# Causal feature-map scores in 64x64 array tiles: only the query columns at or after each 64-key block, new PSUM banks and engine orders

## The reference

```python
x = x + tanh(g_xattn) * performer(layernorm(x), ctx, ctx)
x = x + tanh(g_ffn) * ffn(layernorm(x))
```

```python
num[t] = sum(k'[s] . q'[t] * v[s] for s <= t)
den[t] = sum(k'[s] . q'[t] for s <= t)
out[t] = num[t] / den[t]
```

## Time and profile before

| | |
|---|---|
| median of 3 runs | 1070.0 us (1068.78 to 1070.27) |
| span of the profiled execution, first to last instruction | 1067.6 us |
| TensorE busy | 1012.6 us, 95% |
| VectorE busy | 961.4 us, 90% |
| ScalarE busy | 758.7 us, 71% |
| GpSimd busy | 752.5 us, 70% |
| TensorE's mean granted clock | 0.997 of full |
| HBM read, written | 28.23 MB, 8.39 MB |

### The profile page before, as it was taken

One profiled execution on the slowest core, in us unless ns is written; L12 is line 12 of the kernel. 1 busy time (PEld: TensorE's weight loads), 2 busy tenths in 40 slices (PEclk: granted clock), 3 DMA queues, 4 the chain that ended last, 5 costly groups with the idle time before them and its releaser, 6 DMA issues.

```text
span 1067.6 us, 32201 instructions
## 1 busy us (share of the span) xinstructions
PE 1012.6 (95%) x12870; PEld 831.4 (78%) x12870; DVE 961.4 (90%) x2176; ACT 758.7 (71%) x1564; POOL 752.5 (70%) x1111
## 2 busy tenths in 40 slices
PE   1568999999999999999999999999999999999998
PEld 0447788788888888888888888888888888888787
DVE  7778888999999999999999999999999999998996
ACT  6678877776677777668777666877766687776541
POOL 4578877787677778767778766777876677787531
PEclk9989999999999999999999999999999999999999
DMA  9501000011000001100100100010111000000000
GB/s 311 169 21 31 12 24 29 31 31 31 23 28 25 22 31 31 32 21 24 29 22 32 32 31 22 21 32 21 32 32 31 22 22 31 22 21 12 12 11 30
DMA packets 38915, 38.67 MB, mean 36 GB/s; under 512 B 3440, under 2 KB 38512, under 8 KB 38768
## 3 DMA queue, kind: packets, MB, share of 16 engines
q1 hardware_dynamic: 38384, 36.59, 10.9%
q0 software_dynamic: 384, 0.04, 0.0%
HBM read 28.23 MB, written 8.39 MB: 34 GB/s over the span
## 4 chain that ended last, share of the span: by engine, by line
PE 87%; DVE 5%; POOL 4%; issue 1%; ACT 1%; DMA 0%; SPq 0%; POOLq 0%; DVEq 0%; ACTq 0%
PE ps L2302 15%; PE ps L2304 14%; PE ps L2303 14%; PE ps L2333 10%; PE ps L2348 9%; PE ps L2341 5%; PE ps L2317 5%; PE ps L2382 3%; PE ps L2373 3%; PE ps L2296 2%; PE ps L2358 2%; DVE hk L1770 2%; PE ps L2366 1%; PE ps L2367 1%; PE ps L2325 1%
## 5 line engine op out<-in xcount | busy, mean ns | idle before, releaser
L1434 DVE SCALAR_TENSOR_TENSOR z<-ps,gate,z 128x256 f32<-128x256 f32 x512 | 238.5, 472 | 37.9 <-PE ps L2304 29.0
L2302 PE MATMUL ps<-we_hi,h_hi 128*128 128x512 f32 (+2 forms) x640 | 240.5, 376 | 0.6 <-DVE z L1434 0.4
L2304 PE MATMUL ps<-we_hi,h_lo 128*128 128x512 f32 (+2 forms) x640 | 224.1, 350 | 0.0
L2303 PE MATMUL ps<-we_lo,h_hi 128*128 128x512 f32 (+2 forms) x640 | 223.7, 349 | 0.0
L2302 PEld LDWEIGHTS ps<-we_hi,h_hi 128*128 128x128 f32 x640 | 120.4, 188 | 36.7 <-issue 12.6
L2333 PE MATMUL ps<-qf,kf 64*128 64x256 f32 x1024 | 129.2, 391 | 9.1 <-POOL kf L549 4.5
L2304 PEld LDWEIGHTS ps<-we_hi,h_lo 128*128 128x128 f32 x640 | 120.2, 188 | 17.1
L2303 PEld LDWEIGHTS ps<-we_lo,h_hi 128*128 128x128 f32 x640 | 120.8, 189 | 11.5
L2333 PEld LDWEIGHTS ps<-qf,kf 64*128 64x128 f32 x1024 | 96.4, 191 | 29.8 <-issue 11.3
L2348 PE MATMUL ps<-att,v 128*32 128x256 f32 (+1 forms) x2048 | 109.0, 329 | 3.1 <-POOL att L540 0.9
L911 ACT ACTIVATE att<-ps 128x512 f32<-128x512 f32 x32 | 19.1, 597 | 116.8 <-PE ps L2333 116.7
(11 more groups left out here) (232 smaller groups left out, 3079.7 us busy)
## 6 DMA issues: line engine op xcount, KB each, us to landing
x_in<-in_x SPq DMA_DIRECT2D x32, 256.0 KB, 2.6
c_in<-in_ctx SPq DMA_DIRECT2D x32, 256.0 KB, 2.6
out<-z SPq DMA_DIRECT2D x32, 256.0 KB, 2.2
c_chunk<-in_ctx SPq DMA_DIRECT2D x14, 512.0 KB, 8.0
stage<-in_L_ffn_We SPq DMA_DIRECT2D x2, 1024.0 KB, 10.0
c_chunk<-in_ctx SPq DMA_DIRECT2D x2, 256.0 KB, 6.5
stage_b<-in_L_ffn_bup SPq DMA_DIRECT2D x1, 256.0 KB, 6.9
stage_q<-in_L_ffn_Wq SPq DMA_DIRECT2D x1, 256.0 KB, 6.4
```

Source lines behind the costliest of these rows:

```text
L1434: return dve.scalar_tensor_tensor(out=z[b % 2][:, t, :], in0=ps[:, bank, offset:offset + D], scalar=gate[:, t, ex:ex + 1], in1=z[b % 2][:, ...
L2302: pe.matmul(out, a_hi(c), b_hi(c), start=(c == 0), stop=False)
L2303: pe.matmul(out, a_hi(c), b_lo(c), start=False, stop=False)
L2304: last = pe.matmul(out, a_lo(c), b_hi(c), start=False, stop=(c == C - 1))
```

## The change

Tokens of a batch lie as two blocks of 128. In the key block 1 the halves are exchanged: partitions 0 to 63 hold keys 192 to 255, partitions 64 to 127 keys 128 to 191. The loads of the context do that (`keys_of`, and three transfers per chunk instead of one), and the triangle `causal` is built to match. `first_keys` and `second_keys` become one function `scores`, called for X00, X01, X11 and X10; Y0 and Y1 are gone. Each matmul takes 64 keys as weights and only the queries from the first of these keys on, in a 64x64 tile whose column half is the one in which its keys lie. Score columns that are no longer written are cleared once (`clear_`), and multiplied away or masked. `BANK` is new throughout, so are all orders and the assignment of steps to semaphores, and many waits now stand only for the batches in which they are written out. `a00_` to `a12_` become two steps each (`a00_` and `b00_`).

```diff
-            def first_keys(b, oct, step, *banks):
+            def scores(oct, step, own_banks, last_banks):
                 for j in range(2):
-                    for half in range(2):
-                        r, pr = slice(M * half, M * half + M), 4 * oct + 2 * step + j
-                        last = pe.matmul(ps[:, banks[half], j * L:(j + 1) * L], kf[r, pr, 0:P], qf[r, pr, :],
-                                         start=True, stop=True)
-                return last
-
-            def second_keys(b, oct, *banks):
-                for j in range(4):
-                    for half in range(2):
-                        r, pr = slice(M * half, M * half + M), 4 * oct + j
-                        last = pe.matmul(ps[:, banks[half], j * P:(j + 1) * P], kf[r, pr, P:L], qf[r, pr, P:L],
-                                         start=True, stop=True)
+                    pr, q = 4 * oct + 2 * step + j, (2 * step + j) * P
+                    for c in range(2):
+                        for half in range(2):
+                            r, k = slice(M * half, M * half + M), M * c
+                            pe.matmul(ps[M * c:M * c + M, own_banks[half], j * L + k:(j + 1) * L], kf[r, pr, k:k + M], qf[r, pr, k:L],
+                                      start=True, stop=True, tile_position=(M * half, M * c))
+                    for c in (1, 0):
+                        for half in range(2):
+                            r, k = slice(M * half, M * half + M), M * (1 - c)
+                            last = pe.matmul(ps[M * c:M * c + M, last_banks[half], q + k:q + P], kf[r, pr, P + M * c:P + M * c + M], qf[r, pr, P + k:L],
+                                             start=True, stop=True, tile_position=(M * half, M * c))
                 return last
...
+            def X11_(b):
+                pe.wait_ge(*at("x000", b))
...
+                if b in (0, 1, 5):
+                    pe.wait_ge(*at("x001", b))
+                scores(1, 1, (BANK["x110"], BANK["x111"]), (BANK["y10"], BANK["y11"])).then_inc(*up("X11", b))
...
+            def X10_(b):
+                pe.wait_ge(*at("x011", b))
+                pe.wait_ge(*at("y00", b))
+                scores(1, 0, (BANK["x100"], BANK["x101"]), (BANK["y10"], BANK["y11"])).then_inc(*up("X10", b))
...
@@ hn_t_
-                if b + 1 < NB:
-                    pe.wait_ge(*at("y10", b + 1))
+                if b >= 1:
+                    pe.wait_ge(*at("ssub", b - 1))
@@ fkp_
+                if b == 5:
+                    pe.wait_ge(*at("a13", b - 5))
                 if b >= 5:
-                    pe.wait_ge(*at("a01", b - 5))
+                    pe.wait_ge(*at("b01", b - 5))
@@ banks
-BANK = dict(stab=0, fk0=6, fk1=4, fk2=3, fk3=7, fq0=0, fq1=2, fq2=4, fq3=1, x000=3, x001=1, x010=0, x011=5,
-            y00=3, y01=7, av0=3, x100=0, x101=2, x110=5, x111=4, y10=1, y11=6, av1=2, nd0=2, nd1=0, ht=1,
-            dn=7, qq=1, kv0=7, kv1=5, s=7, pv0=0, pv1=1, otr=4, o=1, h20=3, h21=6, mm0g=3, mm1g=6, mm00=5,
-            mm01=3, mm02=5, mm03=5, mm10=4, mm11=6, mm12=2, mm13=5, first=0)
+BANK = dict(av0=0, av1=3, dn=5, first=0, fk0=0, fk1=6, fk2=4, fk3=5, fq0=2, fq1=3, fq2=7, fq3=4, h20=1, h21=0, ht=2,
+            kv0=2, kv1=6, mm00=4, mm01=0, mm02=7, mm03=7, mm0g=1, mm10=5, mm11=6, mm12=3, mm13=6, mm1g=0, nd0=2,
+            nd1=3, o=7, otr=4, pv0=1, pv1=2, qq=7, s=2, stab=0, x000=1, x001=7, x010=2, x011=4, x100=4, x101=5,
+            x110=3, x111=7, y00=5, y01=0, y10=1, y11=6)
@@ loads
+        def keys_of(dram, b, c):
+            return dram[b, :, :].rearrange("(q p) d -> p q d", p=M)[:, c:4 - c:3 - 2 * c, :]
...
-                sp.dma_start(c_in[b % 2][:, :, :], rows(ctx_d, b)).then_inc(*c_load.up(b))
+                for c in range(2):
+                    sp.dma_start(c_in[b % 2][M * c:M * c + M, :, :], keys_of(ctx_d, b, c)).then_inc(*c_load.up(b))
...
-                sp.dma_start(c_chunk[(b + 1) % CHUNK_BUFFERS][:, 0:n * T, :], rows(ctx_d, at_, n)).then_inc(*ctx_in.up(b))
+                held = c_chunk[(b + 1) % CHUNK_BUFFERS][:, 0:n * T, :].rearrange("p (b t) d -> p b t d", t=T)
+                src = ctx_d[at_:at_ + n, :, :].rearrange("b (q p) d -> p q b d", p=M)
+                sp.dma_start(held[:, :, 0, :], ctx_d[at_:at_ + n, 0:P, :].rearrange("b p d -> p b d")).then_inc(*ctx_in.up(b))
+                for c in range(2):
+                    sp.dma_start(held[M * c:M * c + M, :, 1, :], src[:, 3 - c]).then_inc(*ctx_in.up(b))
@@ gated sums, one of six
-                gated(b, 0, 0, BANK["mm00"], 0).then_inc(*up("a00_", b))
-                dve.wait_ge(*at("a00_", b))
-                gated(b, 0, 1, BANK["mm00"], D).then_inc(*up("a00", b))
+                gated(b, 0, 0, BANK["mm00"], 0).then_inc(*up("a00", b))
+
+            @per_batch
+            def b00_(b):
+                dve.wait_ge(*at("a00", b))
+                gated(b, 0, 1, BANK["mm00"], D).then_inc(*up("b00", b))
@@ once, on VectorE
+            def clear_():
+                for bank in sorted(set(range(8)) - {BANK[f"f{of}{j}"] for of in "kq" for j in range(4)}):
+                    last = dve.memset(ps[:, bank, :], 0.0)
+                last.then_inc(*up("clear"))
```

2045 lines of the change are left out of this document (1084 added, 961 removed).

## The result

The changed kernel takes **1104.6 us** (median of 4 runs, 1101.9 to 1105.4); the kernel before, beside it, 1069.8 (1068.8 to 1070.3). The ratio is **1.0322, 95% interval [1.0308, 1.0337]**: 3.2% slower, where 1050.6 us and a gain of 1.8% were forecast.

What follows compares the result with a forecast made beforehand. TensorE was taken to bound the middle, with VectorE nearest. Gains of 15.6 (24 periods), 3.2 (seven before) and 0.65 (last block) made 19.4 us off the 1067.6 us span; plus 2.4 outside it, 1050.6 us, range 1038 to 1065.

Steps and rivals of the forecast that it cites:

- The other blocks of TensorE keep their matmuls ... nothing: TensorE outside the score block: same matmuls, seven changes of tile shape before and after, so no change in time.
- a gain of 19.4 us: Whole span: 15.6 us from 24 periods, 3.2 from the seven before them, 0.65 from the last block.
- X11, `hn_t` and the feature products had cover: Three places in each period where a possible wait was said to be covered by 0.2 to 0.5 us.
- `hn_t`'s cover of 0.5 us: New wait of `hn_t` on `ssub`, sharing bank 2: VectorE's chain ends at 9.7 us, `hn_t` stands at 10.27.
- The premise behind the sum: 24 middle batches: TensorE's savings shorten the 31.22 us period until another engine blocks, nearest VectorE at about 29.8.
- The sum of the score block: X00's start to `av0`: 4.45 + 0.1 + 0.25 + 0.2 = 5.0 us against 5.64, gain used 0.65 a batch.
- (b): Score block: tiles of unequal length do not run four wide, 0.85 us a batch slower, 1097 us; chance 0.08.
- (c): Score block: weight loads show, 1.75 us a batch, net 1.1 us slower, 1105 us; chance 0.02.
- The start: Up to the first score block: 34 more SyncE transfers, booked at 0, bounds -1 and +3 us.
- a first score block after 43 us: Sign that the forecast is wrong; the first score block was expected within 38 to 42 us.
- The fill: Seven periods before the steady ones: 7 x 0.65 x 0.7 = 3.2 us gained.
- Rival (a): Each period: waits eat part of the gain, 0.48 us left, 1055.5 us; 1070 if nothing is left; chance 0.13.

Runs made afterwards that it cites:

- new_order_wide_tiles: Changed kernel with its new orders, banks and loads, but scores again in two-wide tiles of 128 keys: 1123.5 us, ratio 1.0512.
- x_in_three: Changed kernel with three buffers for x instead of two, its load waiting for `x1` of three batches back: 1097.8 us, ratio 1.0263.
- tiles_in_old_order: Kernel before with only the four-wide score tiles, exchanged key halves and two-transfer key loads, old orders and banks kept: 1070.3 us, ratio 1.0012.
- one_load_a_chunk: Changed kernel with each chunk of keys for the norms loaded by one transfer instead of three, halves exchanged once afterwards: 1101.7 us, ratio 1.0306.
- start_vector_list: Changed kernel with one transfer per chunk and the hand-written start lists of GpSimd and VectorE reordered: 1094.7 us, ratio 1.0246.
- masks-first runs: GpSimd's masks moved ahead of `v_bd` in the old orders, with the new tiles and in the kernel before: 1102.2 and 1101.5 us.

## Why the prediction was wrong

**The step that failed** is the price of what else was changed: "The other blocks of TensorE keep their matmuls ... nothing", with no loss booked for waits and 0 for the start. It priced new orders, banks and waits by counting work. With the loads and the start they cost 52.7 us of span with the old tiles (new_order_wide_tiles), 19.6 of it in the 24 periods, against a gain of 19.4 us that the forecast made of the tiles. The prediction listed where X11, `hn_t` and the feature products had cover, and named no chain ahead of X00. There the bias add, the copy of v and `k_lo` (1.27 + 0.56 + 1.12 us in the chain above) stand on GpSimd between `down_v` and the last feature step. `hn_t`'s cover of 0.5 us was gone in 7 periods of 24, since x came late on VectorE (x_in_three shows it): its load waits for `x1`, two batches back, and such a period is about 0.8 us longer than the others.

**The premise behind the sum failed too**, and alone it would have made the forecast wrong by 20 us: "whatever TensorE is spared comes off the period until another engine is in the way", with VectorE at 29.8 us as the nearest. It weighed busy times of engines. tiles_in_old_order is the clean test: 0.37 us of work less, 0.01 us more of period. What was in the way was no engine but a loop over several, each with idle time. TensorE's own 31.19 us and the loop through GpSimd's masks, 31.23 us with the new tiles, lie on top of each other, and the earlier trace rows could hardly show it, since a loop of the same length as TensorE's work causes almost no wait. The prediction had the end of that loop among its rows: it read that `av0` starts 0.06 us after the mask ends (514.87 and 514.81), and booked 0.2 us there for the change of tile shape.

**The sum of the score block was right**: 4.88 us measured for 5.0, with X11 0.3 us late for 0.25, close to four tiles wide. Its worth too, once it lies in the loop: 18.9 us between new_order_wide_tiles and the changed kernel, for 19.4. That the sums come so near is partly luck: between the two profiles the 24 periods make 13.5 us for 15.6, the fill 2.4 for 3.2, the tail 2.5 for 0.65, and the start is 1.2 us worse, together 17.2 us of span. Rivals (b) and (c) are refuted by the timeline, though their times, 1097 and 1105 us, are close to the measured one: the right number with the wrong reason. One count of the prediction is wrong: a block has 16 instructions a pair and 8 pairs, so 128 and not 256 (4096 in the trace for 32 batches). By the Trainium skill (TensorEngine Tiling (Array Packing), Performance Considerations), 60 cycles each make that 3.2 us, an estimate from that page and not 6.4; it is less than the block's columns need, so a block of 4.88 us neither bears the rule out nor refutes it. Only the head scores speak against it, with 64 instructions in 0.89 us, 14 ns each. By the Trainium skill (TensorE: Matmul & The Clock Gate, Part 3), the two column tiles of a head would not load under each other's matmuls; at 0.55 us a pair for 0.525 of columns, no such load (0.055 us in each of four steps, by the prediction's estimate) shows here either.

**VectorE** needs less, as forecast (28.1 us busy a period for 28.9), and it changed nothing.

**The start** was booked at 0 with +3 as its bound; it is +9.5, and a first score block after 43 us was one of the prediction's own signs of being wrong. Two terms were mis-sized. Issues of 0.47 us were those of batches and chunks in one piece; a part of a split chunk takes 0.60 us, with 0.04 between two, 1.93 us for a chunk where 1.4 was reckoned. And the split data move at 248 GB/s, 2.1 us for a chunk where 1.5 was read. Which of the two holds the start was not separated; with one transfer for each chunk both are gone (342 GB/s from 8 to 24 us), and that is worth 3.0 us of the 9.5 (one_load_a_chunk). Another 2.3 lie in VectorE's and GpSimd's hand-written lists (start_vector_list); 4.2 are unexplained. **The fill** was booked at 3.2 us of gain; 4.8 of the 18.9 us of loss lie in VectorE's list, none in the tiles (188.8 us in the old orders), the cause of the others was not found.

**Rival (a)**, waits that eat part, had the right kind of cause and 0.13. It was bounded by "nothing is left", 1070 us. New orders can cost more than the edit gives; that bound was a further error, and the range, to 1065 us, ended short even of it.

## What to carry to other kernels

Where an engine is busy for 99.9% of a stretch, ask which loops are almost as long: follow the chain of waits once round a period, through all engines, and price the edit by whether that loop passes through it. When the orders change too, walk each new list from what ends a long wait to what TensorE needs next, and count what stands in between on each queue, SyncE's included; the largest wait (here 135.6 us at `q_lo`) may be slack, and the small one in front of the full engine the loop. Look at the gaps of that engine below 0.15 us too, where they always stand at the same step. In three experiments here a step moved out of the way made another late and cost 32 to 121 us, where at most 18 were to be gained: who waits for a moved step, or queues behind it, belongs in the sum.

## What the runs showed of the hardware

- Issues on SyncE: the first seven of the kernel before, of 256 and 512 KB in one piece, took 0.44 to 0.51 us each, one behind another. In the changed kernel, where a chunk is loaded in three parts, most took 0.59 to 0.61 us, with 0.04 us between two. The data of the split chunks moved at 248 GB/s (8 to 24 us), where it was 350 before and 342 in one_load_a_chunk, and the DMA engines were as busy as before (0.99 and 1.01 over the first 40 us).
- Four 64x64 tiles of unequal length run close to four wide: 0.55 us a pair for 0.525 us of columns.
- The masks-first runs: two kernels, 0.15 us of TensorE's work apart, agree to 0.01 us in their period.
